# A tuned decoder layer on one core: four copies of the transposed k go from VectorE to ScalarE, and the engines get new orders

## What is computed

```python
x = x + attn(layernorm(x), Wqkv, Wo)          # 16 heads of 16, RoPE on q and k, causal softmax
x = x + xattn(layernorm(x), ctx, mask)        # scores = x @ ctx.T / 16, masked softmax, @ ctx
x = x + ffn(layernorm(x), gate_w, w1, w2, w3, sw1, sw2, sw3)

# attn
q, k, v = heads(x @ Wqkv);  q, k = rope(q), rope(k)
attn = softmax(where(causal, q @ k.T / 4, -inf));  out = (attn @ v) @ Wo
# ffn: 8 experts of 176, all computed, the 2 best by softmax(x @ gate_w.T) weighted in,
# and a shared one of 352
h = silu(x @ w1.T) * (x @ w2.T);  y = sum_e comb[e] * (h_e @ w3_e.T) + shared
```

## Time and profile before

| | |
|---|---|
| median of 3 runs | 272.88 us (272.65 to 274.71) |
| profiled execution, its own time | 272.15 us |
| its span in the trace | 270.3 us |
| PE busy, matmul records | 257.3 us, 95% |
| ACT, DVE, POOL busy | 174.0, 166.3, 119.2 us |
| granted PE clock | 0.9 or more of full in all 40 slices |

### The profile page before, as it was taken

One profiled execution on the slowest core, in us unless ns is written; L12 is line 12 of the kernel. 1 busy time (PEld: TensorE's weight loads), 2 busy tenths in 40 slices (PEclk: granted clock), 3 DMA queues, 4 the chain that ended last, 5 costly groups with the idle time before them and its releaser, 6 DMA issues.

```text
span 270.3 us, 4890 instructions
## 1 busy us (share of the span) xinstructions
PE 257.3 (95%) x1806; PEld 209.2 (77%) x1806; DVE 166.3 (62%) x361; ACT 174.0 (64%) x290; POOL 119.2 (44%) x133
## 2 busy tenths in 40 slices
PE   7799999999999999959999999999999999999994
PEld 2467666777876888847788988888989898888884
DVE  3388984878778758856452678453755634545463
ACT  7478669979878998979789667536555313223230
POOL 4457915895398897967567453051500000000000
PEclk9999999999999999999999999999999999999999
DMA  7891000000000028000019700000000279000002
GB/s 243 326 397 70 0 2 1 4 2 2 2 0 0 5 79 274 2 5 0 4 49 266 192 1 2 1 0 2 0 0 2 79 168 247 16 0 4 0 0 78
DMA packets 11878, 17.08 MB, mean 63 GB/s; under 512 B 1904, under 2 KB 8272, under 8 KB 11856
## 3 DMA queue, kind: packets, MB, share of 16 engines
q1 hardware_dynamic: 11856, 16.78, 20.1%
...
## 4 chain that ended last, share of the span: by engine, by line
PE 84%; DMA 5%; DVE 4%; ACT 3%; SPq 1%; issue 1%; POOL 1%; DVEq 0%; ACTq 0%
PE bank L776 31%; PE bank L885 14%; PE bank L789 12%; PE bank L938 4%; PE bank L830 4%; DMA res<-x 3%; PE bank L816 3%; PE bank L854 3%; PE bank L783 3%; PE bank L834 3%; PE bank L809 3%; DVE negm L602 2%; PE bank L811 1%; PE bank L818 1%; DMA q_t<-negm_t 1%
## 5 line engine op out<-in xcount | busy, mean ns | idle before, releaser
L408 POOL TENSOR_TENSOR prob_lo<-prob,prob_hi 128x1536 f16<-128x1536 f32 x16 | 49.9, 3121 | 17.4 <-ACT prob_hi L529 17.4
L776 PE MATMUL bank<-x_hi,w_hi 128*128 128x512 f32 x112 | 45.5, 407 | 0.0
L776 PE MATMUL bank<-x_hi,w_lo 128*128 128x512 f32 x112 | 44.2, 395 | 0.0
L776 PE MATMUL bank<-x_lo,w_hi 128*128 128x512 f32 x112 | 44.1, 393 | 0.0
L602 DVE TENSOR_REDUCE negm<-bank 128x2 f32<-128x512 f32 (+1 forms) x48 | 31.5, 687 | 7.0 <-PE bank L811 4.0
L758 DVE TENSOR_TENSOR h_lo<-h_c,h_hi 128x512 fp32r<-128x512 f32 x28 | 19.9, 714 | 23.5 <-ACT h_hi L568 23.4
L744 DVE TENSOR_TENSOR h_c<-bank,h_s 128x512 f32<-128x512 f32 x28 | 19.3, 689 | 24.5 <-PE bank L776 19.8
L562 ACT ACTIVATE h_s<-bank 128x512 f32<-128x512 f32 x28 | 16.7, 598 | 26.2 <-PE bank L776 26.1
L885 PE MATMUL bank<-w_hi,h_hi 128*128 128x256 f32 x112 | 32.8, 293 | 0.1
L568 ACT CAST h_hi<-h_c 128x512 fp32r<-128x512 f32 x28 | 17.2, 616 | 23.5 <-DVE h_c L753 14.0
L885 PE MATMUL bank<-w_lo,h_hi 128*128 128x256 f32 x112 | 31.6, 282 | 0.0
(11 more groups left out here) (128 smaller groups left out, 566.1 us busy)
## 6 DMA issues: line engine op xcount, KB each, us to landing
...
```

The source lines that it names most:

```text
L408: eng.tensor_tensor(prob_lo[:, b % 2], prob[:, b % 2], prob_hi[:, b % 2], ALU.subtract)\
L776: ins = pe.matmul(dst, a(k), c(k), start=(k == 0 and i == 0), stop=(k == kt - 1 and i == 2))
```

## The change

The first batch's four transposes of k (`tr.2`, `tr.3`, `tr.6`, `tr.7`) are copied by ACT in one instruction each, and count in a semaphore of their own, `ka_ok`. DVE's steps `kt.2`, `kt.3`, `kt.6` and `kt.7` are gone; the other twelve copies stay, and the waits for them count four fewer. The table `ORDER` is new for all five engines, with the same steps otherwise; the idle products on PE go from 11 + 3 (`early`, `late`) to 15 + 5.

```diff
     "PE": """
-        xt.0 qk.0 qk.1 v.0 xt.1 qk.2 tr.0 tr.1 v.1 tr.2 tr.3 qk.3 tr.4 m.0 tr.5 m.1 tr.6 m.2 tr.7 m.3 xt.2
+        xt.0 qk.0 qk.1 v.0 xt.1 early.4 tr.0 tr.1 qk.2 tr.2 early.3 tr.3 tr.4 m.0 tr.5 m.1 tr.6 m.2 tr.7 m.3
...
-                    pairs = slice(4 * c, 4 * c + 4)
-                    st = ps_st[c][:].rearrange("p (j q) -> p j q", j=4)
-                    act.copy(q_t[0:SLOT, n // NT % 2, pairs, 0, tok], st[0:SLOT])
-                    act.copy(q_t[SLOT:SHIFT, n // NT % 2, pairs, 1, tok], st[SLOT:SHIFT]).then_inc(s["qt_ok"], 1)
+                    st = ps_st[c % 2][:].rearrange("p (j q) -> p j q", j=4)
+                    pairs = slice(4 * (c % 2), 4 * (c % 2) + 4)
+                    if c < 2:
+                        act.copy(q_t[0:SLOT, n // NT % 2, pairs, 0, tok], st[0:SLOT])
+                        act.copy(q_t[SLOT:SHIFT, n // NT % 2, pairs, 1, tok], st[SLOT:SHIFT]).then_inc(s["qt_ok"], 1)
+                    else:
+                        act.copy(k_t[:, n // NT % 2, pairs, tok], st).then_inc(s["ka_ok"], 1)
...
                     if c >= 2:
                         pe.wait_ge(s["qt_ok"], 2 * n + c - 1)
+                    elif n > NT:
+                        pe.wait_ge(s["kt_ok"], 2 * (n - 1 - NT) + c + 1)
                     elif n:
-                        pe.wait_ge(s["kt_ok"], 2 * (n - 1) + c + 1)
+                        pe.wait_ge(s["ka_ok"], 2 * (n - 1) + c + 1)
...
                     elif b % FILLS == 0:
                         pe.wait_ge(s["qt_ok"], 2 * NT * (b // FILLS + 1))
-                        pe.wait_ge(s["kt_ok"], 2 * NT * (b // FILLS + 1))
+                        pe.wait_ge(s["kt_ok"], 2 * NT * (b // FILLS))
```

More of the change, by code:

```diff
@@ new lines @@
+        ln1n.3 ln2n.0 s.19 t2.0 h.5 xt.3 s.20 h.6 xs.0 pt.0 s.21 w12.4 sh.6 s.22 s.23 h.7 ln3n.0 mt.2 w12.5 t3.0
+        tr.24 sh.7 lg.0 s.24 s.25 w12.6 tr.25 s.26 ct.0 w12.7 ot.1 v.3 tr.28 s.27 tr.29 s.28 s.29 h.8 ln2n.1 h.9
+        t2.1 s.30 vm.3 s.31 w12.8 xs.1 s.32 s.33 pt.1 h.10 w12.9 mt.3 s.34 s.35 h.11 s.36 ln3n.1 s.37 t3.1 s.38 w3.0
+        s.39 w12.10 s.40 lg.1 s.41 up.0 h.12 dn.0 ct.1 w3.1 h.13 up.1 ot.2 s.42 s.43 s.44 s.45 dn.1 s.46 w3.2 up.2
+        ln2n.2 dn.2 t2.2 s.47 w3.3 w12.11 xs.2 h.14 up.3 w3.4 pt.2 h.15 up.4 w12.12 dn.3 up.5 ln3n.2 w3.5 up.6 t3.2
@@ new lines @@
+        m.10 m.11 v.1 kt.10 kt.11 vm.1 qk.4 kt.14 kt.15 m.12 m.13 m.14 m.15 m.16 m.17 m.18 pv.0 m.19 m.20 m.21 m.22
+        m.23 pv.1 qk.5 pv.2 kt.18 pv.3 on.0 kt.19 v.2 wo.0 ln2.0 kt.22 kt.23 vm.2 m.24 m.25 m.26 pv.4 m.27 xs.0 m.28
+        m.29 xc.0 qk.6 m.30 m.31 pv.5 ro.0 ln3.0 m.32 m.33 m.34 m.35 pv.6 qk.7 t3.0 pv.7 lg.0 rk.0 on.1 kt.26 kt.27
+        wo.1 ln2.1 kt.30 kt.31 m.36 m.37 m.38 m.39 m.40 v.3 m.41 xs.1 m.42 m.43 m.44 m.45 m.46 xc.1 m.47 pv.8 ro.1
+        ln3.1 pv.9 pv.10 t3.1 lg.1 rk.1 up.0 pv.11 on.2 vm.3 pv.12 dn.0 wo.2 up.1 ln2.2 dn.1 up.2 dn.2 xs.2 pv.13
@@ L100 @@
-        up.10 xs.3 up.11 pt.3 dn.8 ro.3 dn.9 dn.10 up.12 t3.3 up.13 dn.11 lg.3 dn.12 dn.13 up.14 ct.3 up.15
-        up.16 dn.14 dn.15 up.17 dn.16 up.18 dn.17 up.19 dn.18 up.20 dn.19 up.21 dn.20 up.22 up.23 dn.21 up.24
-        dn.22 dn.23 up.25 up.26 up.27 dn.24 dn.25 dn.26 dn.27
+        xt.0 qk.0 qk.1 v.0 xt.1 early.4 tr.0 tr.1 qk.2 tr.2 early.3 tr.3 tr.4 m.0 tr.5 m.1 tr.6 m.2 tr.7 m.3
+        qk.3 m.4 m.5 v.1 m.6 m.7 xt.2 m.8 m.9 early.1 m.10 m.11 early.3 mt.0 tr.8 tr.9 qk.4 tr.10 s.0 tr.11 s.1
@@ new lines @@
+        tr.12 s.2 tr.13 s.3 early.1 tr.14 early.2 tr.15 s.4 early.1 m.12 m.13 s.5 m.14 m.15 s.6 m.16 s.7 m.17
+        m.18 pv.0 m.19 s.8 m.20 s.9 m.21 s.10 m.22 m.23 s.11 pv.1 mt.1 qk.5 tr.16 tr.17 s.12 pv.2 s.13 tr.18
+        s.14 pv.3 tr.19 s.15 s.16 v.2 ot.0 tr.20 tr.21 wo.0 s.17 tr.22 tr.23 s.18 pv.4 s.19 s.20 m.24 m.25 xt.3
+        t2.0 m.26 s.21 m.27 xs.0 m.28 m.29 qk.6 m.30 pt.0 m.31 pv.5 ro.0 s.22 m.32 m.33 s.23 qk.7 m.34 m.35 pv.6
+        mt.2 t3.0 tr.24 tr.25 pv.7 lg.0 s.24 s.25 v.3 s.26 tr.26 ct.0 tr.27 ot.1 s.27 tr.28 wo.1 tr.29 s.28 s.29
@@ new lines @@
+        tr.30 tr.31 s.30 s.31 m.36 m.37 late.1 m.38 m.39 t2.1 m.40 m.41 xs.1 m.42 m.43 s.32 s.33 pv.8 m.44 m.45
+        pt.1 m.46 m.47 ro.1 mt.3 s.34 s.35 pv.9 s.36 s.37 pv.10 s.38 late.1 t3.1 s.39 late.3 s.40 lg.1 s.41 up.0
+        s.42 pv.11 ct.1 up.1 ot.2 s.43 pv.12 wo.2 s.44 s.45 pv.13 s.46 up.2 s.47 dn.0 t2.2 dn.1 xs.2 dn.2 up.3
+        pt.2 up.4 ro.2 pv.14 up.5 up.6 t3.2 pv.15 dn.3 lg.2 dn.4 up.7 up.8 ct.2 dn.5 ot.3 dn.6 wo.3 up.9 up.10
+        t2.3 dn.7 xs.3 dn.8 up.11 pt.3 dn.9 ro.3 up.12 up.13 t3.3 dn.10 dn.11 lg.3 dn.12 dn.13 up.14 ct.3 up.15
@@ L103 @@
+        up.16 dn.14 dn.15 up.17 dn.16 up.18 dn.17 up.19 dn.18 up.20 dn.19 up.21 dn.20 up.22 dn.21 up.23 dn.22
+        up.24 dn.23 up.25 up.26 up.27 dn.24 dn.25 dn.26 dn.27
     """,
```

60 lines of the change are left out of this document (20 added, 40 removed).

## The result

The changed kernel is slower: 274.27 us (median of 20, 272.45 to 275.99) against 272.71 us for before (median of 20, 271.03 to 274.71). The ratio is 1.0062, with an interval of 1.0042 to 1.0081. That is inside the 1% called "no change" and inside the predicted range. But the predicted sign was a small gain: the sum went down by 0.3 us, the measurement up by 1.6.

What follows compares the result with a forecast made beforehand. TensorE was taken as the bound, gapless from 137 us, so only the four rounds ahead could win. The profiled 272.15 us less 0.3 gave 271.85, plus 0.73 to the median: 272.6 us, range 269.7 to 275.2.

Steps and rivals of the forecast that it cites:

- The moved copies: Four k copies: VectorE loses 2.7 us, ACT gains 2.4 at 0.60 each; the exchange itself gives nothing.
- First round: Up to `mt.0`: `m.0` comes 1.7 us earlier, VectorE's list spends the lead, `mt.0` at 34.75, +0.35 us.
- rival (c): First round: moved memsets hold up GpSimd's `qk.0` and `qk.1`, +1.8 us at `tr.0`, about 274.2 us; chance 0.06.
- Second round: `mt.1` at 54.4, 3.0 us earlier, but GpSimd's `h` steps spend it: `wo.0` at 65.15 against 64.98.
- Rival (a): Second round's lead kept, up to 3.0 us, if ACT reaches `h.2` earlier: 269.7 us; chance 0.20.
- Third round: `h.6` ahead of `qk.6` on GpSimd: `mt.2` at 87.5, +0.85 us; gate product behind `pv.7` at 90.6, +1.7.
- Rival (b): GpSimd's queue, `h.6` and `h.7` ahead, ends the third round late, through to `s.36`: 275.7 us; chance 0.14.
- Fourth round: `mt.3` at 115.1, +0.2 us, `s.36` at 118.95, `up.0` about 125.1; with `pv.11` still to do, +0.8 in all.
- Rival (d): Shift DMA landing, binding at batch 3, moves the time by -0.9 to +0.7 us; counted inside the 0.60 case.
- To the end: From `up.0` on: 0.9 us of slack and 0.2 for one idle product fewer turn +0.8 into -0.3 us.
- signs of being wrong: `h.3` ending before 59, `mt.3` before 113.5 or after 116.5, first `rot` clearly over 1.3 us, wait over 1 us after 137.
- The base: Starting time: the profiled execution of before, 272.15 us, with 0.73 us added to reach the median.

Runs made afterwards that it cites:

- e8: Kernel before with only the four k copies moved to ACT, and 13 idle products filling the wait ahead of `s.36`: 271.99 us, ratio 0.9987.
- e12: e9 with `v.0` on VectorE ahead of `m.0` instead of behind it: 272.78 us, ratio 1.0009.
- e13: e12 with `qk.3` on VectorE moved behind `m.11` and `v.1`, and `sh.3` on ACT behind `tr.9`: 274.00 us, ratio 1.0067.
- e11: e1 with the two q_t memsets moved back on VectorE behind `m.11`, ahead of `v.1`: 278.27 us, ratio 1.0208.
- e10: e1 with third-round `h.6`, `h.7` on GpSimd and `pv.6`, `pv.7` on TensorE and VectorE back in their places of before: 276.13 us, ratio 1.0129.
- e2: Kernel before with 13 idle products filling TensorE's wait ahead of `s.36`: 271.80 us, ratio 0.9993.
- e14: The kernel of e2, unaltered, measured again: 272.07 us, ratio 0.999.
- e1: Changed kernel with eight more idle products in TensorE's wait ahead of `s.36`: 273.31 us, ratio 1.004.
- e6: e1 with `pv.11` put back from behind `up.0` to ahead of `lg.1`, in place of three idle products: 273.90 us, ratio 1.0066.
- e9: e1 with VectorE's `dn.0` behind `up.1` and `wo.2`, and `dn.10`, `dn.11` ahead of `ro.3` and `ln3.3`: 272.43 us, ratio 0.999.
- e15: Changed kernel, unaltered, measured again: 273.29 us, ratio 1.0041.
- e16: e9 with ACT's `sh.0` ahead of `w12.2` and `ln1n.1` ahead of `w12.0`: 272.56 us, ratio 1.0001.

## Why the prediction was right or wrong

*The moved copies.* Right. Four copies on ACT at 592 ns, predicted 0.60, and e8 shows them to be worth nothing in the orders of before, as the sum had it:

```profile
L513 ACT CAST k_t<-bank 128x512 fp32r<-128x512 f32 x4 | 2.2, 592 | 0.2
```

*First round.* The number was right, the reason at best half right, so that the hit was in part luck. I had 34.75 for `mt.0` by VectorE's list of maxima and three steps among them; it came at 34.82. But e12 and e13 took two of those steps out of the list and `mt.0` stood still after `m.0`: TensorE's own list was as long. I had added one engine's queue and never the other's, because TensorE's waits are small in the earlier trace rows, and that is what one sees when two lists keep pace. I also had not seen that the new order on ACT hangs the round on the load of w1. The memsets were free, as said (e11), and rival (c) falls: GpSimd's `qk.0` and `qk.1` took 1.28 and 1.27 us beside them. Here the Trainium skill's rule (SBUF - State Buffer, Who interferes with whom) held. These are GpSimd's first steps and the memsets in after:

```profile
12.60 1.28 POOL L388 TENSOR_TENSOR rot<-rope_c,rope_s 128x512 f32<-128x512 f32 x1 [2.58 <-DVE rope_s L645]
16.26 1.27 POOL L388 TENSOR_TENSOR rot<-rope_c,rope_s 128x512 f32<-128x512 f32 x1
...
12.89 1.76 DVE L619 MEMSET q_t<- 64x2048 f32 x1 [0.37 <-issue]
16.34 1.76 DVE L619 MEMSET q_t<- 64x2048 f32 x1 [0.48 <-issue]
```

*Second round.* Right in kind: `mt.1` 2.45 us earlier, all gone by `wo.0` over GpSimd's closed loop of `h` steps, whose `h.3` ended at 60.48 (60.05 predicted). That the `h` steps are what spent the lead is read from the trace; no run moved them alone. Rival (a), the lead kept, falls.

*Third round.* The times were near (87.66 and 90.38), the cause was not: with `h.6` put back (e10) `mt.2` did not move, so its nearness was luck, and what made it late is open. Rival (b) named this queue as the loss; e10 shows it to be a gain, and `wo.1` came at 97.50, ahead of the 99 from which (b) would decide.

*Fourth round.* +0.4 instead of +0.2 at `s.36`. Over the profiles `mt.3` lies between 114.5 and 114.9 us with before's order (before, e2, e8, e14), between 114.9 and 115.4 with after's (after, e1, e6, e9, e15), and at 116.57 in e12, where w1 landed late. Rival (d) is part of every execution: from `mt.3` to `s.36` it took 2.93 to 4.30 us over all profiles, so this copy and its DMA move one execution by more than the whole loss ahead of them.

*To the end.* This is the step that failed. I let 0.9 us of slack behind `up.0` take `pv.11` and the lateness, took 0.2 off for an idle product, and counted -0.3 in all. Measured with the clock left out (e1), `lg.3` stands 1.5 us later than in before. `s.44` and `lg.3` in before, and then in e1:

```profile
135.01 0.50 PE L830 MATMUL bank<-q_t,k_t 113*128 113x256 f32 x2
...
202.73 0.17 PE L776 MATMUL bank<-gate_hi,x_hi 128*128 128x8 f32 x1
```
```profile
135.52 0.50 PE L832 MATMUL bank<-q_t,k_t 113*128 113x256 f32 x2
...
204.25 0.17 PE L778 MATMUL bank<-gate_hi,x_hi 128*128 128x8 f32 x1
```

`pv.11` was taken (e1 at `s.44`: +0.51 against +0.46 at `s.36`, with `pv.11` done and an idle product fewer; e6 agrees). The lateness was not, and 1.0 us came on top behind `s.44`, at the two meetings of VectorE and GpSimd, the larger part of which e9 removed. The sum had no term for such meetings: it costed each instruction at its mean length in before, though the new orders put it beside other work. I had quoted the half of the rule that clears the memsets, and did not ask which instructions with two SBUF inputs would now run beside GpSimd. The Trainium skill (SBUF - State Buffer, Who interferes with whom) says that such a VectorE instruction contends with GpSimd instructions that read SBUF; the trace agrees (1.97 us for 0.68). None of the prediction's signs of being wrong came (`h.3` ended at 60.48, `mt.3` started at 115.29, the first `rot` took 1.28 us, TensorE's longest wait after 137 us was 0.3), since none of them looked at VectorE beside GpSimd.

*The base.* The sum started from a profiled execution at full clock and was lifted by 0.73 us to the median, as if that were noise. It is a mixture of two kinds 1.5 us apart. Within a kind the change costs 1.5 to 1.7 us: 0.9 at the meetings (e1 to e9), 0.5 that remain (e9 at 272.43 against 271.89 for e2 and e14), and 0.1 to 0.3 in scatter. Of the 0.5, the traces of e9 and e14 show 0.15 behind `s.44` (from there to `lg.3` 67.90 against 67.74 us). By the ratios to before beside them (0.999 for e9, 0.9993 and 0.999 for e2 and e14) there is nothing left to explain, but these divide by a mixture. The rest lies ahead of `s.36` and is open: the landing of w1 fits its size, but e16, which took it out, had no better median.

No version beats before clearly. The fastest, e2, e8 and e14, stand at 0.999 with 1 inside all three intervals.
